# Attention and a mixture of experts: routed experts on gathered rows, expert work between attention slots

## The chip, the core and the metric

The kernel runs on one core of one Trainium2 chip. The metric is the device time of one execution in microseconds (us). Engines: PE multiplies matrices, DVE, ACT and POOL work element by element, SP issues DMAs.

## What is computed

The input is 4 batches of 1024 tokens, 256 wide (4096 tokens). Attention has 16 heads of 16; a query sees every key up to 64 places after itself. Each token then goes through a router that chooses 4 of 16 experts, and 2 shared experts.

```
x = layernorm(x + attention(x))              # 16 heads, key <= query + 64
scores = sigmoid(x @ router.T); sc = scores + bias
# 2 of 4 groups by the sum of their two best sc, then the 4 best experts in them
tw = scores[chosen] / sum * 2.5
routed = sum over chosen e of tw_e * (silu(x @ G_e.T) * (x @ U_e.T)) @ D_e.T   # 256 -> 128 -> 256
shared = (silu(x @ SG.T) * (x @ SU.T)) @ SD.T                                  # 256 -> 256 -> 256
out = layernorm(x + routed + shared)
```

## The kernel before

Matrix products at full precision are made of three products of 16-bit floats (high by high, high by low, low by high), with weights scaled by 64. Each engine has its own instruction list, and the lists meet at semaphores.

**Projection** (`project`, L631): eight chunks of 512 tokens. PE makes q, k and v (L647, L651); q and k are written to DRAM in two halves (L324) and read back in stacked form for each group of four heads (`stack`, L326 to L336). v stays in SBUF.

**Attention**: 16 groups (4 batches, 4 head groups), each of 13 slots (`SLOTS`, L34: a query half of 512 and a key tile of 128). In a slot PE makes the transposed scores of four heads (L587), ACT their exponential (L863), POOL cuts the masked corner (L509), and PE multiplies by v one slot later, four heads at once, in 32-bit floats (`weighted`, L604). Between them PE makes the untransposed scores of the next group (L572, L575), of which DVE takes row maxima (L984). The maxima are transposed (L616) and put into the q stack by a DMA, so that the exponential needs no bias. Scores have three PSUM banks, transposed scores three, P times V one, and transposes one (L252). The first part of `body` on every engine writes this order out by hand; `share` (L61) deals the score units to the slots. The weights of one expert are loaded and split in each group (L340, L853, L1010).

**Expert stage**: eight chunks of 512 tokens after all attention. All 18 experts are computed for all tokens: `up` (L750) makes gate and up in 12 matmuls of 512 columns each, ACT the silu (L940), DVE multiplies by the token's weight for that expert, which is 0 where it isn't chosen and comes broadcast from DRAM (L1185, L417), and by up (L1192); ACT and DVE split the result (L947, L1199); `down` (L764) adds 12 matmuls of 256 columns into two banks. The steps of the next chunk (`STEPS`, L283) stand between the experts: output projection (L680, L688), first norm, transposes (L696), logits (L704), routing (`route`, L1090, a chain of 30 small DVE operations, each waiting for the one before), and the transpose of the weights (L712). After the last expert come the residual (L1207) and the second norm. Loops over chunks and groups are hardware loops (`rounds`, L80).

## Time and profile before

| | |
|---|---|
| median of 3 runs | 1291.25 us (1289.18 to 1295.77) |
| profiled execution, span | 1287.9 us (3.35 below the median; its own device time is not listed) |
| instructions | 28066 |
| DMA | 76.78 MB, mean 60 GB/s |

The span runs from the first to the last instruction. Busy times of PE are not work at its peak, since matmuls are pipelined and their ends are modelled; spacing from start to start says more. The clock of PE is given as a share of 2.4 GHz.

### The profile page before, as it was taken

The page shows a single profiled execution, that of the slowest core. Times are in us where ns is not written, and L with a number is a line of the kernel's source. Part 1 is how long each engine was busy: PE and PEld are TensorE (multiplying, and loading weights), DVE is VectorE, ACT ScalarE, POOL GpSimd, SP SyncE. Part 2 cuts the span into 40 slices and gives each one's busy share as a digit, 9 for nine tenths or more (in the row PEclk, how much of TensorE's full clock was granted, in tenths as well). Part 3 has the DMA queues.
Part 4 walks back from the last instruction along what each step waited for, and adds up shares of the span by engine and source line. Part 5 has one row for each costly group of instructions (what it writes and reads, how often), then busy time and mean ns, then how long its engine had stood idle before and what let it go on. Part 6 is the DMA issues. An engine that isn't in the chain of part 4 may idle for free.

```text
span 1287.9 us, 28066 instructions
## 1 busy us (share of the span) xinstructions
PE 1214.8 (94%) x8448; PEld 644.6 (50%) x8448; DVE 947.5 (74%) x1975; ACT 625.9 (49%) x1366; POOL 238.9 (19%) x432
## 2 busy tenths in 40 slices
PE   7877999999999999999799999898998989989997
PEld 4543444444444444443356666565665656556564
DVE  7587888888888888887657776676776767757754
ACT  4415777777777777777633332323222232222332
POOL 8831222222222222222401010010200102000000
PEclk9998999999999999999999999898999999999999
DMA  5631111111111111110131232121312212122220
GB/s 166 187 116 53 38 39 39 37 37 37 37 37 37 37 34 32 34 36 14 46 84 61 48 99 59 61 71 43 90 49 63 77 51 90 50 47 77 59 82 33
DMA packets 62443, 76.78 MB, mean 60 GB/s; under 512 B 8992, under 2 KB 37408, under 8 KB 62368
## 3 DMA queue, kind: packets, MB, share of 16 engines
q1 hardware_dynamic: 60736, 72.80, 19.2%
q10 hardware_dynamic: 1632, 3.15, 0.8%
q8 instruction: 27, 0.44, 0.2%
q14 instruction: 48, 0.39, 0.1%
HBM read 62.94 MB, written 12.85 MB: 59 GB/s over the span
## 4 chain that ended last, share of the span: by engine, by line
PE 64%; DVE 13%; issue 9%; ACT 7%; SPq 2%; POOL 2%; DMA 2%; DVEq 0%; ACTq 0%; POOLq 0%
PE bank L759 16%; PE bank L604 11%; PE bank L572 9%; PE bank L587 9%; PE bank L772 9%; DVE hf L1192 3%; DVE sg L1185 3%; ACT hh L947 3%; ACT a_PT L863 3%; PE bank L647 2%; PE bank L575 2%; PE bank L688 1%; PE bank L628 1%; PE bank L651 1%; SPq L324 1%
## 5 line engine op out<-in xcount | busy, mean ns | idle before, releaser
L984 DVE TENSOR_REDUCE a_mx<-bank 128x1 f32<-128x512 f32 (+3 forms) x720 | 401.2, 618 | 73.7 <-PE bank L575 44.6
L863 ACT ACTIVATE a_PT<-bank 128x512 f32<-128x512 f32 (+4 forms) x832 | 357.0, 505 | 138.1 <-PE bank L587 137.5
L587 PE MATMUL bank<-a_QS,a_KS 113*128 113x512 f16 (+4 forms) x832 | 269.6, 331 | 11.4 <-ACT a_PT L863 6.1
L572 PE MATMUL bank<-a_KS,a_QS 112*128 112x512 f16 (+4 forms) x832 | 258.6, 332 | 15.5 <-DVE a_mx L984 8.3
L947 ACT CAST hh<-hf 128x512 f16<-128x512 f32 x144 | 89.0, 618 | 332.5 <-DVE hf L1192 332.5
L509 POOL TENSOR_SCALAR_AFFINE_SELECT a_PT<-a_PT 128x256 f32<-128x256 f32 (+1 forms) x288 | 109.6, 381 | 419.0 <-ACT a_PT L863 418.7
L604 PE MATMUL bank<-a_PT,a_VG 128*17 128x512 f32 (+4 forms) x1664 | 179.7, 504 | 6.4 <-POOL a_PT L509 6.4
L772 PE MATMUL bank<-dh,hh 128*128 128x256 f16 x576 | 159.0, 276 | 16.9 <-DVE z L1207 16.9
L1199 DVE TENSOR_TENSOR hl<-hf,hh 128x512 f16<-128x512 f32 x144 | 99.8, 693 | 99.4 <-ACT hh L947 99.4
L772 PE MATMUL bank<-dh,hl 128*128 128x256 f16 x576 | 159.1, 276 | 0.0
L772 PE MATMUL bank<-dl,hh 128*128 128x256 f16 x576 | 159.1, 276 | 0.0
L572 PEld LDWEIGHTS bank<-a_KS,a_QS 112*128 112x128 f16 x832 | 79.4, 98 | 114.6 <-DVE a_mx L984 84.2
L587 PEld LDWEIGHTS bank<-a_QS,a_KS 113*128 113x128 f16 x832 | 80.0, 98 | 109.4 <-ACT a_PT L863 54.8
L1192 DVE SCALAR_TENSOR_TENSOR hf<-bank,sg 128x512 f32<-128x512 f32 x144 | 99.5, 691 | 42.9 <-issue 28.5
L940 ACT ACTIVATE sg<-bank 128x512 f32<-128x512 f32 x144 | 85.6, 594 | 89.9 <-PE bank L759 89.9
L1185 DVE TENSOR_TENSOR sg<-sg,cb 128x512 f32<-128x512 f32 x128 | 91.0, 711 | 36.7 <-ACT sg L940 31.2
L575 PE MATMUL bank<-a_tri,a_idb 128*128 128x128 f16 (+1 forms) x576 | 111.3, 212 | 0.0
L523 POOL TENSOR_SCALAR ve<-mv 128x4 f32<-128x4 f32 x16 | 6.4, 402 | 545.2 <-DVE mv L1052 545.2
L759 PE MATMUL bank<-x1h,gh 128*128 (+1 forms) x288 | 87.3, 385 | 0.7 <-ACT cT L904 0.7
L759 PE MATMUL bank<-x1h,uh 128*128 (+1 forms) x288 | 86.0, 380 | 1.6 <-DVE hf L1192 1.6
L759 PE MATMUL bank<-x1l,gh 128*128 (+1 forms) x288 | 86.8, 384 | 0.0
L759 PE MATMUL bank<-x1h,gl 128*128 (+1 forms) x288 | 86.2, 381 | 0.0
(134 smaller groups left out, 1438.2 us busy)
## 6 DMA issues: line engine op xcount, KB each, us to landing
cb<-c_dram SPq DMA_DIRECT2D x128, 256.0 KB, 3.3
q_dram<-p_qk SPq DMA_DIRECT2D x32, 128.0 KB, 2.1
k_dram<-p_qk SPq DMA_DIRECT2D x32, 128.0 KB, 2.1
a_QS<-q_dram SPq DMA_DIRECT2D x64, 64.0 KB
a_KS<-k_dram SPq DMA_DIRECT2D x64, 64.0 KB
xb<-x SPq DMA_DIRECT2D x8, 512.0 KB, 3.6
out<-oo SPq DMA_DIRECT2D x8, 512.0 KB, 4.2
p_xf<-xT ACTq DMA_DIRECT2D x6, 512.0 KB, 4.2
```

The lines of the kernel that those rows point to most:

```text
L509: pool.affine_select(out=a, in_=a, compare_op=ALU.is_ge, fill=0.0, base=q0 - (kt * P - WIN), pattern=[[0, 2], [1, w]], channel_multiplier= ...
L572: mm = pe.matmul(bank[:, at:at + hi - lo], QS[p][0:MR, t // NT, h, t % NT * P:t % NT * P + P], KS[p][0:MR, piece, h % 2, 0:hi - lo], start ...
L575: mm = pe.matmul(bank[:, at + m0 - lo:at + hi - lo], idb[:], tri[:, m0 - P * t - WIN:m1 - P * t - WIN], start=False, stop=True)
L587: pe.matmul(stbank[u % 3][:, 0:(qc + 1) * CH - q0], KS[p][0:MR + 1, kt // NT, h % 2, kt % NT * P:kt % NT * P + P], QS[p][0:MR + 1, qc, h, ...
L604: mm = pe.matmul(otbank[32 * h:32 * h + HD + 1, q0 - qc * CH:CH], VG[p][:, kt, h:VW:HG], PT[(p + i) % 2][:, h, 0:(qc + 1) * CH - q0], star ...
L759: mm = pe.matmul(bank[:], ww[:, k, n, :], xx[:, k, bass.ds(t * CH, CH)], start=(i == 0), stop=(i == 5))
L772: mm = pe.matmul(y, a[n % NHB][:, j * P:j * P + P], w[:, n, :], start=(n == 0 and i == 0 and j % 2 == 0), stop=(n == NX - 1 and i == 2), s ...
L863: act.activation(PT[(p + i) % 2][:, h, 0:w], stbank[u % 3][:, 0:w], ACT.Exp)\
L947: act.copy(hh[n % NHB][:], hf[n % 2][:]).then_inc(f["hi_done"], 1)
L984: dve.tensor_reduce(mx[:, piece, t // NT, heads[0]:heads[0] + n, t % NT], sbank[u % 3][:, 0:n * w].rearrange("p (h k) -> p h k", h=n), AX. ...
L1185: dve.tensor_tensor(sg[n % 2][:], sg[n % 2][:], cb[e % NCB][:], op=ALU.mult)\
L1192: dve.scalar_tensor_tensor(hf[n % 2][:], ubank[n % 2][:], 1.0 / WSC, sg[n % 2][:], op0=ALU.mult, op1=ALU.mult).then_inc(f["h_done"], 1)
```

## The change

Only the order of the work and the routed experts change; projection and attention compute what they did, with v written to DRAM after the projection and read back per group.

**Order.** All hardware loops are unrolled. A function `plan` gives each engine a table of jobs by half slot (26 per attention group, 416 for all attention, 602 in all). PE takes at most one job in a half slot; the other engines may have several. A job is issued in the middle and at the end of each attention slot (`fill`). Batch b's side work begins at half slot 104 x (b + 1), when its attention is done; what is beyond 416 follows after attention. By the plan, preparation of batches 0 to 3 (output projection, norm, transposes, logits, routing, positions) stands at half slots 106 to 142, 210 to 246, 314 to 350 and 418 to 453; scatters at 143 to 163, 247 to 267, 351 to 371, 454 to 474; the 24 routed pairs at 170 to 269, 293 to 392, 421 to 486, 506 to 560; the 8 shared items at 125 to 146, 271 to 290, 396 to 414, 488 to 504; gathers at 282 to 302, 404 to 424, 498 to 518, 572 to 592. Pairs are three half slots apart within attention (more where PE's are taken) and two after it.

**Routed experts.** For each batch, `route` ends with the rank of each expert; PE counts positions by 44 matmuls with triangular and full matrices of ones; DVE (`place`, a chain of 18 operations) gives every token four row numbers, in expert order, each expert's rows padded to a multiple of 128: 48 units of 128 rows, whatever the routing. 32 indirect DMAs on POOL's queue write token rows (512 16-bit values, high and low part) to those rows in DRAM. Units are worked off in pairs: a transposing DMA loads 256 rows (256 KB, three buffers), PE reads the units' expert numbers into registers (8 at a time) and makes gate and up in 24 matmuls of 128 columns, weights addressed by register; ACT takes tanh, DVE makes the gated product in two operations, ACT and POOL split it, PE makes the output in 6 matmuls of 256 columns, ACT copies it out and SP stores it to DRAM (256 KB). 32 indirect DMAs on POOL's queue gather the four rows of each token, DVE adds them with their weights (32 dependent operations), and the second norm follows. Shared experts work on 256 tokens at a time with static weights.

**Memory.** The banks for scores and transposed scores become one ring of five taken in PE's order (0 to 4); P times V keeps bank 6, and banks 5 and 7 serve everything else; after attention a ring of seven serves all. Weights are loaded and split in the first six groups, three per group, by one operation each instead of three. `normal` scales four tiles in one operation instead of four.

The core of the diff:

```diff
+UNITS_B = TOPK * S // P + NE
+NPR = UNITS_B // 2
+NPS = NSH * NT
+NPB = NPR + NPS
...
+for b in range(B):
+    h0 = span * (b + 1)
+    for half in range(NH2):
+        c = b * NH2 + half
+        e = h0 + (2 if half == 0 else 7)
+        sp[e - 1].append(("load_res", c))
+        pool[e + 4].append(("add_bo", c))
+        o = e - 1
+        for k in range(KD):
+            o = put(("ont", c, k), o + 1)
+            act[o + 1].append(("oh", c, k))
+            dve[o + 2].append(("ol", c, k))
+        y = o + 2
+        for j in range(2):
+            y = put(("yo", c, j), y + 1)
+            dve[y + 1].append(("z", c, j))
+            dve[y + 2].append(("stats", c, j))
+        dve[y + 3].append(("aggr", c))
+        pool[y + 4].append(("rstd", c))
+        dve[y + 6].append(("norm", c))
+        act[y + 7].append(("row_hi", c))
+        pool[y + 8].append(("row_lo", c))
...
+q = -1
+for b in range(B):
+    for n in range(NPB):
+        shared = n < NPS
+        if shared:
+            h = ready[b * NH2 + n // NPS * NH2 + n // (NPS // 2)] if n else ready[b * NH2]
+            h = max(h, q + 2)
+        else:
+            h = max(routed[b] + 6, q + (3 if q < 2 * ATT else 2))
+        q = put(("gu", b, n), h)
+        act[q + 1].append(("tanh", b, n))
+        dve[q + 2].append(("gate", b, n))
+        act[q + 3].append(("hh", b, n))
+        pool[q + 4].append(("hl", b, n))
+        if not shared:
+            sp[q - 5].append(("load_rows", b, n))
+            y = put(("y", b, n), q + 6)
+            act[y + 1].append(("y_out", b, n))
+            sp[y + 3].append(("store_y", b, n))
+        elif n % NSH:
+            y = put(("ysh", b, n), q + 6)
+            dve[y + 1].append(("add_shared", b, n))
+    at = y + 6
+    for t in range(BT):
+        for k in range(TOPK):
+            pool[at + (t * TOPK + k) * 2 // 3].append(("gather", b, t, k))
+        w = at + (t * TOPK + TOPK) * 2 // 3 + 3
+        dve[w].append(("combine", b, t))
+        dve[w + 1].append(("stats2", b, t))
+        if t % NT == NT - 1:
+            c = b * NH2 + t // NT
+            dve[w + 2].append(("aggr2", c))
+            pool[w + 3].append(("rstd2", c))
+            dve[w + 4].append(("norm2", c))
+            sp[w + 5].append(("store", c))
...
+def take(ring, *job):
+    at = RINGS[ring][turn[ring] % len(RINGS[ring])]
+    turn[ring] += 1
+    if at in holder:
+        on.wait_ge(*emptied(holder[at]))
+    holder[at], bank_of[job] = job, at
+    return banks[at]
...
+        i = routed_nth(b, n)
+        u = 2 * (n - NPS)
+        if u % REGS == 0:
+            load_experts(b, u)
+        on.wait_ge(xt_loaded[i % 3], i // 3 * 16 + 16)
+        on.wait_ge(s["w_lo"], NX)
+        cols = [(experts[b, u + v], v * P, P,
+                 [(xt[i % 3][:, k, v * P:v * P + P], xt[i % 3][:, KD + k, v * P:v * P + P])
+                  for k in range(KD)]) for v in range(2)]
+    ps = take(ring, "gu", b, n)
+    for e, at, v, tall in cols:
+        for up in range(2):
+            i = 0
+            for lo, part in ((0, 0), (0, 1), (1, 0)):
+                for k in range(KD):
+                    mm = pe.matmul(ps[:, up * 2 * P + at:up * 2 * P + at + v],
+                                   weights(e, (2 * up + lo) * D + k * P, P), tall[k][part],
+                                   start=(i == 0), stop=(i == 5))
+                    i += 1
+    mm.then_inc(f["gu_ready"], 1)
+elif what == "y":
+    b, n = a
+    q, u = nth(b, n), 2 * (n - NPS)
+    on.wait_ge(f["hl_done"], q + 1)
+    ps = take(ring, "y", b, n)
+    for v in range(2):
+        e = experts[b, u + v]
+        for i, (o, at) in enumerate(((hh, 4 * D), (hh, 5 * D), (hl, 4 * D))):
+            mm = pe.matmul(ps[:, v * D:v * D + D], o[q % 4][:, v * P:v * P + P], weights(e, at, D),
+                           start=(i == 0), stop=(i == 2))
+    mm.then_inc(f["y_ready"], 1)
...
+sp.dma_start_transpose(xt[i % 3][:], rows[b % 2][at:at + 2 * P, :])\
+  .then_inc(xt_loaded[i % 3], 16)
...
+pool.indirect_dma_start(rows[b % 2], bass.IndirectOffsetOnAxis(ap=slot[b % 2][:, t, k:k + 1],
+                        axis=0), XR[:, t, :], None).then_inc(f["scattered"], 16)
...
+elif what == "gather":
+    b, t, k = a
+    i = b * BT + t
+    for n in range(3):
+        on.wait_ge(y_stored[n], (b + 1) * NPR // 3 * 16)
+    on.wait_ge(f["comb_done"], i - 1)
+    pool.indirect_dma_start(yg[i % 2][:, k, :], None, outs[b % 2], bass.IndirectOffsetOnAxis(
+        ap=slot[b % 2][:, t, k:k + 1], axis=0)).then_inc(gathered[i % 2], 16)
...
+elif what == "gate":
+    q = nth(*a)
+    ps = bank("gu", *a)
+    on.wait_ge(f["tanh_done"], q + 1)
+    dve.scalar_tensor_tensor(ga[q % 2][:], tq[q % 2][:], 1.0, ps[:, 0:2 * P], op0=ALU.add,
+                             op1=ALU.mult).then_inc(f["ga_done"], 1)
+    on.wait_ge(f["ga_done"], q + 1)
+    on.wait_ge(f["hl_done"], q - 1)
+    dve.scalar_tensor_tensor(hf[q % 2][:], ps[:, 2 * P:4 * P], 0.5 / WSC / WSC, ga[q % 2][:],
+                             op0=ALU.mult, op1=ALU.mult).then_inc(f["h_done"], 1)
...
+    ins = dve.scalar_tensor_tensor(zz, yg[i % 2][:, k, :], wk[b % 2][:, t, k:k + 1], zz,
+                                   op0=ALU.mult, op1=ALU.add)
+    ins.then_inc(f["comb_step"], 1)
+    on.wait_ge(f["comb_step"], i * TOPK + k + 1)
+dve.sem_inc(f["comb_done"], 1)
...
+for G in range(NR):
+    def some_scores(units):
...
+    for i in range(NSL):
+        rest, h2 = share(i), 2 * (G * NSL + i)
+        for h in range(HG):
+            scoresT(G, i, h)
+            some_scores(rest[h:h + 1] if h < HG - 1 else ())
+            if h == 1:
+                fill(h2)
+        if i:
+            weighted(G, i - 1)
+        some_scores(rest[HG - 1:])
+        if i == NSL - 1:
+            weighted(G, i)
+        fill(h2 + 1)
+for h in range(2 * ATT, END):
+    fill(h)
```

## Rows read from the trace of the kernel before

**Rows 1.** The page's busy line: busy us, share of the span, instructions per engine.

```profile
PE 1214.8 (94%) x8448; PEld 644.6 (50%) x8448; DVE 947.5 (74%) x1975; ACT 625.9 (49%) x1366; POOL 238.9 (19%) x432
```

**Rows 2.** Windows by stage: us; busy us (instructions) PE, PEld, DVE, ACT, POOL; clock, DMA, GB/s.

```profile
160.44:193.70 33.26, 32.80 (x257) 13.85 (x255) 27.64 (x60) 24.38 (x59) 7.25 (x19) 1.00 0.13 37
644.80:1287.90 643.10, 613.38 (x3936) 378.66 (x3936) 437.33 (x894) 198.63 (x360) 50.00 (x62) 0.98 0.23 65
```

**Rows 3.** Chain of waits in the expert stage: start us, us, what, how many.

```profile
656.63 1.31 PE bank L772 x12
657.94 0.87 PE bank L680 x8
658.82 2.59 PE bank L759 x12
...
662.72 2.62 PE bank L688 x24
...
685.71 0.59 PE bank L704 x24
```

**Rows 4.** PE in order of time, in the second attention group: start us, us, what.

```profile
195.21 0.22 PE L575 MATMUL bank<-a_tri,a_idb 128*128 128x128 f16 x1
195.27 0.38 PE L587 MATMUL bank<-a_QS,a_KS 113*128 113x512 f16 x1
195.58 1.07 PE L604 MATMUL bank<-a_PT,a_VG 128*17 128x512 f32 x8
196.58 0.31 PE L572 MATMUL bank<-a_KS,a_QS 112*128 112x320 f16 x1
```

**Rows 5.** DVE by line and form, 150 to 600 us: busy us, mean ns; idle before.

```profile
L984 DVE TENSOR_REDUCE a_mx<-bank 128x1 f32<-128x512 f32 x328 | 208.8, 683 | 38.7 <-PE bank L572 26.3 <-PE bank L575 12.4
```

**Rows 6.** Waits between 160 and 600 us: us in total, times, longest.

```profile
PEld bank L572 <- DVE a_mx L984: 64.8, 106, 0.8
```

**Rows 7.** SP's queue in order of time; the page's DMA issues (KB each, us to landing).

```profile
60.44 1.21 SPq L324 DMA_DIRECT2D k_dram<-p_qk  x2
68.50 0.75 SPq L334 DMA_DIRECT2D a_QS<-q_dram  x1
...
cb<-c_dram SPq DMA_DIRECT2D x128, 256.0 KB, 3.3
q_dram<-p_qk SPq DMA_DIRECT2D x32, 128.0 KB, 2.1
```

**Rows 8.** DVE in order of time: routing of chunk 0, and four statistics.

```profile
632.82 0.20 DVE L1105 TENSOR_SCALAR th<-th 128x64 f32<-128x64 f32 x1 [2.10 <-ACT th L899]
...
643.39 0.44 DVE L1141 SCALAR_TENSOR_TENSOR vm<-rank,th 128x64 f32<-128x64 f32 x1
...
828.00 1.40 DVE L1048 BATCH_NORM_STATS2 st<-z 128x6 f32<-128x256 f32 x4
```

**Rows 9.** DVE by line and form, 740 to 1200 us: 512 and 256 elements.

```profile
L1069 DVE SCALAR_TENSOR_TENSOR z<-bank,xb 128x512 f32<-128x512 f32 x12 | 7.7, 686 | 5.9 <-PE bank L688 5.9
...
L1207 DVE SCALAR_TENSOR_TENSOR z<-bank,o_all 128x256 f32<-128x256 f32 x20 | 7.1, 417 | 0.0
```

**Rows 10.** POOL by line and form: 150 to 600, 636 to 646, 740 to 1200 us.

```profile
L509 POOL TENSOR_SCALAR_AFFINE_SELECT a_PT<-a_PT 128x256 f32<-128x256 f32 x159 | 64.8, 408 | 110.9 <-ACT a_PT L863 110.9
...
L509 POOL TENSOR_SCALAR_AFFINE_SELECT a_PT<-a_PT 128x256 f32<-128x256 f32 x6 | 4.8, 830 | 2.2 <-ACT a_PT L863 2.2
...
L517 POOL TENSOR_TENSOR xb<-xb,bo 128x256 f32<-128x256 f32 x20 | 16.1, 835 | 0.0
```

**Rows 11.** Chain of waits during the projection: start us, us, what.

```profile
44.97 5.31 issue
...
103.55 4.30 DMA a_KS<-k_dram
```

**Rows 12.** Register operations on PE's queue at the logits: duration ns min/median/max.

```profile
L704 PEldq FUSED_REGOPS  x13: 46/46/51, 760.0 to 843.7; - x13
```

1583 lines of the change are left out of this document (850 added, 733 removed).

## Prediction

> **What bounds the kernel now.** I read the page's busy line first: PE 1214.8 of 1287.9 us, DVE 947.5 [rows 1]. Then the windows by stage. One attention group takes 33.3 us (16 of them, 108 to 642 us), with PE busy 32.8, DVE 27.6, ACT 24.4, POOL 7.3; the expert stage takes 643.1 us with PE busy 613.4 and DVE 437.3 [rows 2]. In the chain of waits of the expert stage PE hardly stops: an expert on 512 tokens costs 2.59 us up and 1.31 us down [rows 3], so 144 of them are 562 us, and the steps of the next chunk make up the rest. In attention PE streams too: a slot's P times V takes 1.00 us, and 128 columns cost 0.06 us from start to start [rows 4]; the score maxima on DVE are 683 ns for 512 columns [rows 5], and PE's weight loads wait 64.8 us of 440 for them [rows 6]. So PE leads in both stages, and in attention DVE is close behind (83%). That decides what follows: PE work is removed, but a large part of what stays is put where PE is already full and DVE nearly so.
>
> **The change, priced part by part.**
>
> *Expert arithmetic.* Routed experts shrink from 128 passes over 512 tokens to 96 pairs of 128-row units (24 per batch; 32 full units of work and 16 for the padding). A pair is 24 matmuls of 128 columns and 6 of 256. From 0.06 us and 1.31/12 = 0.109 us [rows 3, 4] that is 24 x 0.056 + 6 x 0.109 = 2.0 us. The 8 expert numbers that PE reads from memory once in four pairs are on no row. Below stands 0 (all hidden), above eight landings one after the other of 2.1 us, 17 us; a small read kept in the engine's own queue is nearest to an issue on SP, 0.75 us [rows 7], so I take 0.8 us, 0.2 per pair: 2.2 us a pair. That makes 96 x 2.2 = 211 us in place of 128 x 3.90 = 499. Shared experts stay 16 x 3.90 = 62 us, 15.6 per batch. The preparation of 1024 tokens is 2 x (0.87 + 2.62 + 0.87 + 0.59) = 9.9 us of PE [rows 3] (transposes, projection, transposes, logits), 11 with the 44 tiny matmuls for the positions.
>
> The Trainium skill ("TensorE: Matmul & The Clock Gate", Back-to-back issue gap) gives about 81 ns for a 128-column matmul in a stream with weight loads, where its isolated gap is 56. The trace speaks against it here: 24 pairs of weight load and 16-column matmul take 0.59 us [rows 3], so a weight load bounds nothing above 25 ns. By the page a pair would cost 0.6 us more, and the sum some 30 us more.
>
> *DVE per batch.* Preparation: Ol, z and x1l are 12 operations of 0.69 us [rows 9]; statistics and norm are 16 of 256 elements at 0.35 us from start to start [rows 8] and 8 small ones, 6.6 us. Two routings keep the chain up to the rank reduction, which ended 10.5 us after the start of the first of now 30 operations (632.82 to 643.39 [rows 8], 25 operations), and one more: 21.5 us. The 18 chained placing operations on up to 768 elements, by 1.05 ns an element and 0.15 us each (417 ns at 256, 686 at 512 [rows 9]), are 8.8 us. Together 45 us. A gate is two operations of 0.4 us: 24 pairs 19 us, 8 shared 6.4, with 2.8 for adding. Combining is 32 dependent operations at 0.44 us, 14 us, and the second norm 6.6. In all some 94 us per batch.
>
> *POOL and the indirect DMAs.* Per batch 32 operations hl of 0.83 us [rows 10] and 32 scatters and 32 gathers of 128 rows each. No row shows an indirect DMA. Bounds: SP spends 0.60 to 0.75 us to issue a direct one; from issue to landing 128 KB take 2.1 us [rows 7]. I take 1.0 us of POOL's queue for each, nearer to the issue, since the engine need not wait for the landing, but above it, since each row's address is worked out on POOL. Range 0.6 to 2.1.
>
> *Transposing loads* (96 of 256 KB) and the stores of y run in SP's queue beside the arithmetic; three buffers ahead. Bounds 0 and the 3.3 us of a 256 KB landing [rows 7], hidden by three buffers as long as each takes less than 3 x 2.2 us. I charge nothing; if the cover is gone, a rival below.
>
> *Start.* Without the loops the pause of 5.31 us in the projection's chain goes [rows 11]. The end of the start is bound by SP's queue and the a_KS landing at 103.55 + 4.30 [rows 11]. Ten weight loads move off that queue, one v store per chunk and one v load are added. I take 97 us in place of 108: the pause and 8 issues of 0.7 us go; bounds 92 and 110.
>
> *Attention with filling.* Engines work in order and PE runs at most five banks ahead, so stretches limited by different engines do not average: I take the largest per stretch. One half slot is 33.3/26 = 1.28 us, of which PE needs 97%, DVE 83%, POOL 0.28 us. By half slots of the plan:
> By half slots of the plan (a stretch of n bare ones is n x 1.28 us, times the engine's share; batch b's side work begins at 104 x (b + 1)):
> - 0 to 104, nothing of weight beside the groups: 133 us.
> - 104 to 143, preparation of batch 0 and 6 shared gates, DVE leads: 41 + 45 + 5 = 91.
> - 143 to 170, scatters: POOL 32 + 6 of masks in 20 half slots, then 7 bare ones, 9: 47.
> - 170 to 210, 11 pairs, PE leads: 50 + 24 = 74.
> - 210 to 247, preparation of batch 1 beside 5 to 7 pairs, DVE leads: 39 + 45 + 6 = 90.
> - 247 to 282, scatters, masks and 5 hl on POOL 42, then 15 half slots with shared experts, 27: 69.
> - 282 to 306, gathers of batch 0: POOL 32 + 6 + 6 for hl, then 5: 49.
> - 306 to 350, preparation of batch 2 and pairs, DVE leads: 47 + 45 + 7 = 99.
> - 350 to 371, scatters, POOL 43. 371 to 396, 7 pairs, PE 46. 396 to 416, shared experts, PE 39.
>
> The sum is 780 us in place of 534.
> The two rings of three banks become one of five: from nothing to 0.1 us in each of 208 slots (the wait for maxima, 64.8 us in 172 slots [rows 6], is 0.38 us per slot now); I take 8 us.
>
> *Tail after attention*, in the same way. All 24 pairs of batch 2 and all of batch 3 are still to do. Preparation of batch 3 with 8 pairs and the rest of batch 1's combining: DVE 45 + 13 + 6, 66 us with gaps. 32 scatters with 10 hl: 40. Six pairs and first shared: 17. Gathers of batch 2 with 10 hl: 40. 17 pairs: 37. Last y landing 4, 32 gathers 32, last combine, norm and store 12: 48. Sum 248 us.
>
> **The sum**: 97 + (780 + 8) + 248 = 1133 us of span. It is made against the profiled span of 1287.9; the median of the runs, 1291.25, lies 3.35 above it, which I add: 1136.
>
> **Rivals.**
> *A. The stretches average out.* PE and DVE queues absorb each other's bursts. Then attention is bound by the sum of DVE, 16 x 27.6 + about 250 = 692 us, with 4% of coupling 720, and POOL's tail overlaps a little more (230): 97 + 720 + 230 + 3 = 1050. For it speaks that the engines' queues already mix two streams at 98% of PE [rows 2]; against it the wait of 0.38 us per slot for maxima at DVE's present load [rows 6].
> *B. PE's pair costs more*, since each weight address comes from a register, and a pair has 28 of them. A register operation in PE's queue takes 46 ns [rows 12]: 1.3 us on top of 2.2. Of 96 pairs some 45 lie where PE leads: 60 us more, 1196. For it: 28 operations beside 60 dispatches in 2.0 us. Against it: logits with such addresses run at 25 ns a matmul [rows 3].
> *C. POOL becomes the bound* (the other side). An indirect DMA keeps POOL for c us; masks stand behind scatters in its queue, PE's P times V waits for the masks, and in the tail three rounds of 32 stand alone. 4.4 rounds in attention and 3 in the tail make 237 x (c - 1) us. It is slower than before from c = 1.65, and 1397 at c = 2.1. For it: masks of 256 elements took 830 ns instead of 408 while DVE did the routing [rows 10], and now eight routings and 128 combines stand near POOL's work. Against it: SP issues in 0.75.
> The Trainium skill ("SBUF — State Buffer", SBUF: two separate sides, and the section after it) says that GpSimd can't write its DMA descriptors while VectorE holds the port pair that both use, and has such a DMA go from some 0.62 to 3.1 us. By that figure for all of them the time would be some 1630 us, an estimate from that page. The slowed masks are of the same kind, at twice the time and not five times.
> *D. The transposing loads are slow.* Above 6.6 us each three buffers no longer hide them; at 8 us, 48 pairs in the tail at 8/3 or, if they don't overlap each other, at 8 us cost 48 x 5.8 = 278 us more: 1414. Slower than before from 5.3 us if they go one by one.
>
> **Chances.** Forecast 0.42, A 0.20, B 0.20, C 0.12 (0.08 of it beyond c = 1.65), D 0.06. A change within 0.5% (6.5 us, about what the three runs' spread of 6.6 us can tell) is left 0.03, the part of C around its point. Slower: 0.08 + 0.06 = 0.14. Faster: the rest, 0.83. Range: A with POOL's c a little under 1.0 reaches 1030 (24 us for 0.1); above it takes B with c at 1.3, 1196 + 71 = 1267, so 1270. That leaves some 0.03 below and 0.15 above.
>
> **What will show it.** The last P times V at about 885 us (97 + 788); indirect DMAs on POOL at 1.0 us from start to start; routed matmuls of 128 columns at 56 ns; group periods that alternate between 33 us at first, and 50 to 65 us where a batch is prepared; DVE above 90% in those, PE above 90% in the routed ones; PE sparse, and its clock at the lower level (1.2 GHz), while POOL scatters and gathers after attention. I am wrong if the period does not grow where batches are prepared (A), if PE's pairs stand over 3 us in a stretch without waits (B), if PE waits for masks or hl behind DMAs (C), or if pairs wait for xt (D).

## The result, and the profile after

The changed kernel takes 1379.27 us (median of 4 runs, 1376.3 to 1383.12) where the kernel before takes 1292.88 in the same job: 1.0678 times as long, interval 1.0648 to 1.0708. It is slower by 6.8%; forecast were 1136 us, range 1030 to 1270. The profiled execution has a span of 1374.6 us against 1287.9. The page's busy line, to be read beside [rows 1]:

```profile
PE 1034.1 (75%) x8592; PEld 603.9 (44%) x8592; DVE 867.9 (63%) x1832; ACT 595.9 (43%) x1361; POOL 582.5 (42%) x807
```

PE is busy for 181 us less. But its share of the span fell from 94% to 75%, and no other engine is full. So the gain went into waits. Where, the windows by stage say (columns as in [rows 2]): a group of attention without side work; half slots 104 to 143, 210 to 247 and 306 to 350 of the plan, in which a batch is prepared and routed; and all that is left behind attention:

```profile
188.70:226.50 37.80, 34.26 (x259) 13.98 (x262) 29.00 (x56) 26.07 (x60) 7.48 (x19) 1.00 0.73 240
263.90:374.70 110.80, 83.22 (x655) 45.29 (x658) 88.67 (x199) 48.21 (x111) 36.14 (x49) 0.85 0.18 50
521.30:634.20 112.90, 84.01 (x727) 49.19 (x727) 81.85 (x188) 46.10 (x108) 35.22 (x49) 0.85 0.28 57
795.90:920.70 124.80, 94.67 (x845) 55.55 (x844) 93.72 (x212) 55.87 (x132) 40.35 (x63) 0.88 0.33 69
1051.00:1374.60 323.60, 183.18 (x1792) 150.21 (x1792) 159.23 (x380) 75.19 (x174) 168.62 (x195) 0.75 0.55 132
```

In the three preparations PE is busy 74 to 76% and DVE 72 to 80%, at a granted clock of 0.85 to 0.88, where a bare group has 1.00. In the first of the three both are busy at once for only 62.6 of 110.8 us, PE alone for 20.6, DVE alone for 26.0, neither for 1.5; in the others both are busy for 55.6 of 112.9 and 66.2 of 124.8. So neither engine leads; they take turns. The waits of the first preparation between the two (us in total, times, longest) are in the main these:

```profile
DVE a_mx L1095 <- PE bank L461: 12.3, 9, 3.6
DVE a_mx L1095 <- PE bank L458: 6.3, 4, 2.8
PE bank L656 <- DVE e_hf L1327: 6.0, 2, 4.8
PE bank L631 <- DVE e_hf L1327: 4.8, 2, 2.7
PE bank L580 <- DVE e_hf L1327: 3.7, 1, 3.7
```

DVE's waits for PE's scores make 18.6 us, PE's for DVE all of its 27.6 us of idle time; e_hf is the gated product of an expert pair, x1l the low half of the normed tokens.

The plan's stretches against the forecast (from the first P times V of a slot to that of another, read in order of time), with two runs from further down. The one without routing also leaves out the indirect DMAs and the reading of expert numbers; of the last version the slowest of four executions was profiled (1273.38 us, the median is 1265.84). By the mark used here the start of the kernel before takes 110.6 us, where the forecast counts 108.

```
us                 forecast  changed  no routing  last version
start                    97    115.6       115.3         115.9
half slots 0-104        133    148.3       147.5         148.4
104-143                  91    110.8        81.1         100.5
143-170                  47     60.6        45.6          46.1
170-210                  74     86.0        76.6          75.7
210-247                  90    112.9        79.2         100.2
247-306                 118    161.7       148.3         137.5
306-350                  99    124.8        93.8         133.6
350-416                 128    130.2       114.4         116.1
rings                     8        -           -             -
behind attention        248    323.6       208.8         297.5
span                   1133   1374.6      1110.6        1271.6
```

How PE and DVE take turns is seen on PE in order of time, at the start of a preparation (in brackets idle time before it, and what ended it):

```profile
305.03 0.96 PE L487 MATMUL bank<-a_PT,a_VG 128*17 128x448 f32 x8
309.68 1.11 PE L580 MATMUL bank<-a_ident,e_R 128*128 128x128 f32 x4 [3.69 <-DVE e_hf L1327]
...
311.33 0.63 PE L458 MATMUL bank<-a_KS,a_QS 112*128 112x512 f16 x1
314.68 0.61 PE L631 MATMUL bank<-e_x1h,a_W 128*128 128x256 f16 x2 [2.71 <-DVE e_x1l L1313]
```

and on DVE in the same microseconds:

```profile
304.36 0.26 DVE L1163 TENSOR_SCALAR e_th<-e_th 128x64 f32<-128x64 f32 x1
...
309.20 0.42 DVE L1327 SCALAR_TENSOR_TENSOR e_hf<-bank,e_ga 128x256 f32<-128x256 f32 x1
311.42 0.69 DVE L1095 TENSOR_REDUCE a_mx<-bank 128x1 f32<-128x512 f32 x1 [1.79 <-PE bank L458]
...
313.93 0.69 DVE L1313 TENSOR_TENSOR e_x1l<-bank,e_x1h 128x512 f16<-128x512 f32 x1
```

The transposes of L580 need one of the two banks that all side work shares, and that bank is free only when DVE has made e_hf from it (L1327). That stands behind 13 routing operations, which began at 304.36, and two maxima. PE is idle for 3.69 us; when it goes on, DVE in turn waits 1.79 us for the scores that PE could not make meanwhile. The next pause has the same shape, with x1l (L1313).

A pair of routed units, in the tail:

```profile
1265.80 1.64 PE L631 MATMUL bank<-e_xt,a_W 128*128 128x128 f16 x23
...
1268.12 2.17 PE L631 MATMUL bank<-e_xt,a_W 128*128 128x128 f16 x24
...
1270.86 0.27 PE L644 MATMUL bank<-a_W,e_hl 128*128 x1
1274.30 0.93 PE L631 MATMUL bank<-e_xt,a_W 128*128 128x128 f16 x8 [3.17 <-issue]
```

One pair takes 2.85 us (from 1268.12 on, the last of its 30 matmuls 0.11 us behind 1270.86), and every four pairs PE stands 3.2 us for "issue", so that a pair costs 3.6. What its queue does in that time is no matmul; by line:

```profile
L535 PEldq FUSED_REGOPS  x192: 146/146/165, 425.6 to 1302.7; - x192
L535 PEldq SEQ_ASSERT  x192: 18/18/24, 425.8 to 1302.9; - x192
L535 PEldq TENSOR_LOAD <-e_expert x24: 587/592/1120, 424.8 to 1299.9; - x24
```

This is the reading of eight expert numbers, each compared with its bound. The same operation as in [rows 12] now stands before two in three of the weight loads of the gate and up matmuls (2304 in all), 46 ns each:

```profile
L631 PEldq FUSED_REGOPS  x1536: 46/46/51, 428.0 to 1313.5; - x192
```

POOL's indirect DMAs (duration min/median/max in ns):

```profile
L916 POOL DMA_INDIRECT rows<-e_XR,e_slot x128: 956/961/1866, 359.0 to 1176.8; - x128
...
L931 POOL DMA_INDIRECT a_pool<-outs,e_slot x128: 940/947/1232, 709.3 to 1361.8; - x128
```

With 31.6 us of issue in 124 places before L916, one comes every 1.25 us. What stood behind them in POOL's queue shows in the waits (us in total, times, longest; a_PT L883 is the masking of the corner, e_hl the low half of the gated product):

```profile
PEld bank L487 <- POOL a_PT L883: 35.3, 29, 5.1
PE bank L644 <- POOL e_hl L923: 28.7, 19, 7.8
...
PE bank L656 <- POOL e_hl L923: 18.7, 5, 4.7
```

At the start the pause of [rows 11] is gone, but in its place the chain of waits runs through the round trip of V by DRAM, and a_KS lands 5 us later than before:

```profile
32.63 5.02 DMA v_dram<-p_vs
...
100.72 3.24 DMA v_dram<-p_vs
108.10 4.74 DMA a_KS<-k_dram
```

### The profile page after: what moved, and what is told of

It reads as the page before. It is cut to its first block, busy times and chain, and to the rows that moved or that the text cites. A ratio compares the mean times of both kernels' runs of the same rounds, so it can differ in the third digit from the quotient of the medians.

```text
span 1374.6 us, 25464 instructions
## 1 busy us (share of the span) xinstructions
PE 1034.1 (75%) x8592; PEld 603.9 (44%) x8592; DVE 867.9 (63%) x1832; ACT 595.9 (43%) x1361; POOL 582.5 (42%) x807
## 4 chain that ended last, share of the span: by engine, by line
PE 40%; DVE 20%; POOL 18%; issue 13%; DMA 3%; SPq 2%; ACT 2%; POOLq 0%; DVEq 0%
PE bank L631 10%; PE bank L487 8%; PE bank L471 7%; POOL a_pool L931 7%; DVE a_mx L1095 6%; PE bank L458 6%; POOL rows L916 6%; PE bank L644 4%; POOL e_hl L923 2%; POOL a_PT L883 2%; DVE e_R L1345 2%; ACT a_PT L992 1%; PE bank L461 1%; SPq L717 1%; PE bank L517 1%
## 5 line engine op out<-in xcount | busy, mean ns | idle before, releaser
L471 PE MATMUL bank<-a_QS,a_KS 113*128 113x512 f16 (+4 forms) x832 | 283.8, 349 | 25.4 <-DVE a_mx L1095 18.8
L883 POOL TENSOR_SCALAR_AFFINE_SELECT a_PT<-a_PT 128x256 f32<-128x256 f32 (+1 forms) x288 | 114.2, 402 | 396.1 <-ACT a_PT L992 395.5
L458 PE MATMUL bank<-a_KS,a_QS 112*128 112x512 f16 (+4 forms) x832 | 270.0, 346 | 12.5 <-DMA a_KS<-k_dram 6.1
L631 PE MATMUL bank<-e_xt,a_W 128*128 128x128 f16 x2304 | 198.0, 244 | 53.2 <-issue 36.3
L631 PEld LDWEIGHTS bank<-e_xt,a_W 128*128 x2304 | 171.8, 109 | 82.6 <-issue 65.0
L923 POOL TENSOR_TENSOR e_hl<-e_hf,e_hh 128x256 f16<-128x256 f32 x128 | 94.1, 736 | 198.6 <-ACT e_hh L1050 197.7
L916 POOL DMA_INDIRECT rows<-e_XR,e_slot x128 | 127.2, 994 | 57.7 <-issue 31.6
L931 POOL DMA_INDIRECT a_pool<-outs,e_slot x128 | 124.1, 970 | 60.5 <-issue 30.5
L471 PEld LDWEIGHTS bank<-a_QS,a_KS 113*128 113x128 f16 x832 | 84.0, 102 | 115.1 <-DVE a_mx L1095 52.9
L458 PEld LDWEIGHTS bank<-a_KS,a_QS 112*128 112x128 f16 x832 | 82.8, 102 | 106.2 <-ACT a_PT L992 64.8
L644 PE MATMUL bank<-a_W,e_hh 128*128 x384 | 80.3, 305 | 61.3 <-POOL e_hl L923 28.7
L1323 DVE SCALAR_TENSOR_TENSOR e_ga<-e_tq,bank 128x256 f32<-128x256 f32 x128 | 53.2, 416 | 104.5 <-ACT e_tq L1043 101.4
L1345 DVE SCALAR_TENSOR_TENSOR e_R<-a_pool,e_wk,e_R 128x256 f32<-128x256 f32 x128 | 69.0, 539 | 44.9 <-DMA a_pool<-outs,e_slot 41.4
L1056 ACT ACTIVATE e_ys<-bank 128x512 f32<-128x512 f32 x96 | 57.5, 599 | 40.4 <-PE bank L644 40.2
L461 PEld LDWEIGHTS bank<-a_tri,a_idb 128*128 128x128 f16 x576 | 57.6, 103 | 31.9 <-issue 9.6
```

Of the source, the lines that this page charges most:

```text
L458: mm = pe.matmul(ps[:, at:at + hi - lo], QS[p][0:MR, t // NT, h, t % NT * P:t % NT * P + P], KS[p][0:MR, piece, h % 2, 0:hi - lo], start=T ...
L461: mm = pe.matmul(ps[:, at + m0 - lo:at + hi - lo], idb[:], tri[:, m0 - P * t - WIN:m1 - P * t - WIN], start=False, stop=True)
L471: pe.matmul(ps[:, 0:(qc + 1) * CH - q0], KS[p][0:MR + 1, kt // NT, h % 2, kt % NT * P:kt % NT * P + P], QS[p][0:MR + 1, qc, h, q0 - qc * C ...
L631: mm = pe.matmul(ps[:, up * 2 * P + at:up * 2 * P + at + v], weights(e, (2 * up + lo) * D + k * P, P), tall[k][part], start=(i == 0), stop ...
L644: mm = pe.matmul(ps[:, v * D:v * D + D], o[q % 4][:, v * P:v * P + P], weights(e, at, D), start=(i == 0), stop=(i == 2))
L883: pool.affine_select(out=a, in_=a, compare_op=ALU.is_ge, fill=0.0, base=q0 - (kt * P - WIN), pattern=[[0, 2], [1, w]], channel_multiplier= ...
```

## The experiments

The trace left three theories. S: PE's side jobs wait for DVE work that stands behind routing in DVE's queue, with two banks for all of them. W: routing is vector work that is paid for in full, however it is placed. C (P in the two runs on the pace of the DMAs; in another expectation P stands for PE as the bound): POOL's indirect DMAs set the pace of what stands behind them. Each kernel was timed in three rounds beside the kernel before (medians of that one: 1289.3 to 1291.5 us). Ratios are to the kernel before, so that the runs of different jobs can be compared; the changed kernel is at 1.0678.

### What each part costs

**Expert numbers.** In `load_experts`:

```diff
-    _, regs = nc.values_load_multi_w_load_instructions(expert[b % 2][0:1, n:n + REGS], ...)
-    for i, e in enumerate(regs):
-        experts[b, n + i] = e
+    for i in range(REGS):
+        experts[b, n + i] = (n + i) % NE
```

> The expert numbers are fixed at build time (unit n uses expert n mod 16), so the load of the numbers into PE's registers, its bounds checks and the address arithmetic per weight load are left out. Theory PE (rival B: the dear routed pair is what the forecast missed): in the changed kernel a pair takes 2.0 us up and 0.8 us down with register addresses, where 1.34 and 0.65 were forecast, and each group of four pairs pays 3.4 us for the load; 96 x 0.9 + 24 x 3.4 = 165 us less PE work, of which at least half is on the path: 1300 us or less. Theory order (the five engines hold each other up in a fixed order, and PE's own work is seldom what ends last): under 50 us, 1330 us or more.

1340.4 us, ratio 1.0369 (1.033 to 1.0407): 39 us, as theory order had it, not PE. A pair takes 2.01 us in its trace (1257.23 to 1259.24 below), as the forecast's 2.0 had it:

```profile
1257.23 1.51 PE L629 MATMUL bank<-e_xt,a_W 128*128 128x128 f16 x24 [0.45 <-DMA e_xt<-rows]
...
1259.24 1.50 PE L629 MATMUL bank<-e_xt,a_W 128*128 128x128 f16 x24
```

So addresses from registers cost 0.85 us a pair and the reading of numbers another 0.8, of which the forecast had 0.2.

**Indirect DMAs.** Scatters and gathers replaced by the bare signal:

```diff
-    pool.indirect_dma_start(rows[b % 2], ..., XR[:, t, :], None).then_inc(f["scattered"], 16)
+    pool.sem_inc(f["scattered"], 16)
-    pool.indirect_dma_start(yg[i % 2][:, k, :], None, outs[b % 2], ...).then_inc(gathered[i % 2], 16)
+    pool.sem_inc(gathered[i % 2], 16)
```

> Scatters and gathers are left out (POOL only counts the semaphores up), so experts work on the zeros in the row buffer and the sum takes what lies in the buffer. Theory POOL (rival C: scatters and gathers at 1.27 us from start to start, 0.98 busy and 0.27 issue, hold the masks and the hl operations up): 7.4 rounds of 32 x 1.27 = 300 us of POOL, of which each round hides at most what the others need, some 22 us: 1379 - 7.4 x 20 = about 1230 us. Theory PE: POOL only fills time that PE's dear pairs need anyway, 1340 us or more.

1294.69 us, 1.0019 (0.9998 to 1.004): 85 us, of them 60 in the tail (323.6 to 263.7). That lies between the two theories. PE's wait for masks falls from 35.3 to 18.7 us and that for e_hl from 28.7 to 6.8.

**Transposing loads.** `dma_start_transpose` became a plain `dma_start` of the same bytes (what the pairs then multiply is not transposed).

> The transposing loads become plain loads of the same 256 KB (the transposition of the gathered rows is left out). Theory D (slow transposing loads): PE waits for them in the tail, 48 pairs by several us: 1280 us or less. All others: within 15 us of the changed kernel, 1365 to 1385 us; SP's issue falls from 1.3 to 0.7 us, which is off the path.

1397.71 us, 1.0819 (1.079 to 1.0848): nothing to gain there. It came out 18 us slower, which neither side expected.

**All of these and routing.** Fixed numbers, no indirect DMAs, and routing and placing left out but for one copy and two fills:

```diff
-    (26 operations per chunk in route, 18 per batch in place)
+    dve.memset(M[:, j0:j0 + NT, :], 0.0).then_inc(f["rank_done"], 1)
+    dve.memset(wk[b % 2][:], 0.0).then_inc(f["wk_done"], 1)
```

> Leaves out the routing and the placing on the vector engine (two small fills and one copy stand for them), all 256 indirect DMAs, and the loading of expert numbers, which are fixed when the kernel is built; every matmul, load, gate and combination is still done. With the second and first experiment (1294.69 and 1340.4 us) it says how much of the change is paid for choosing and moving tokens and how much for the pairs themselves. If what each leaves out adds up, no indirect DMAs (-84) and fixed numbers (-39) give 1256; theory W (routing fills the vector engine in the half slots 104 to 143, 210 to 247 and 306 to 350, 349 us against 147 before): another 60 to 100 us off, 1160 to 1200. Theory M (the pairs' own matmuls, gates and transposing loads fill these half slots): within 20 us of 1256.

> Leaves out the 256 indirect DMAs and fixes the expert numbers when the kernel is built; routing and placing are still computed. It stands between the run without the indirect DMAs (1294.69 us) and the one that also leaves routing out (1108.86). If the prices add up (39 us for the numbers), 1256 us, and routing and placing then cost 147 us, more than the 119 us of vector work that they are. If TensorE bounds what is left once POOL is relieved, the numbers cost more than 39 here: 1210 to 1240.

Without routing 1108.86 us, 0.8585 (0.8562 to 0.8608), below all that was expected. With routing, but with fixed numbers and no indirect DMAs, 1219.97, 0.9449 (0.9417 to 0.948). The prices don't add up: fixed numbers give 39 us alone and 75 beside relieved POOL. And routing costs 111 us (1219.97 - 1108.86) where its own DVE time is 858.4 - 748.7 = 110 us. The preparation 104 to 143, first with routing, then without:

```profile
264.40:376.80 112.40, 83.35 (x651) 44.88 (x650) 88.46 (x198) 48.03 (x110) 30.55 (x44) 0.85 0.16 43
```

```profile
262.80:343.90 81.10, 72.04 (x651) 40.90 (x650) 60.82 (x131) 47.25 (x110) 26.66 (x44) 0.98 0.21 59
```

DVE has 27.6 us more to do, the stretch takes 31.3 longer, and PE's same 651 instructions are busy for 83.4 in place of 72.0 us: the granted clock went from 0.98 to 0.85 as PE came to stand idle. None of the routing is hidden, though DVE is at 79%. Together with it, though, its chain of dependent steps was left out, on which scatters and pairs wait; the pair of runs doesn't tell the two apart.

### In what way routing costs

**Banks.** Two rings for the scores, `"scores": [0, 1, 2], "scoresT": [3, 4]`; then six banks for the first four groups and one for the rest of their work:

```diff
-RINGS = {"scores": [0, 1, 2, 3, 4],
+RINGS = {"scores": [0, 1, 2, 3, 4], "early": [0, 1, 2], "earlyT": [3, 4, 5], "one": [7],
```

> Same computation; scores get a ring of banks 0 to 2 of their own and transposed scores banks 3 and 4, in place of one ring of five in PE's order. Theory ring: in the first groups, which have no side work, the period grew from 33.3 to 37 us because transposed scores now wait for maxima on DVE and scores for exponentials; with rings of their own it falls to 34 us or less there, and the time by 16 x 3 = 50 us, to 1330. Rival (the DMA traffic and the weight splits of the first groups did it): period stays at 36 us or more, time within 10 us of 1379.

> Same computation. In the first four attention groups, where no routed work runs, the scores get six banks in two rings of three, as the kernel before has them, and everything else one bank; from the fifth group on it is the changed kernel. Theory B (the lost bank and the shared ring cost the 37.4 us per group against 33.3): the first four groups fall from 148.3 to 134 to 138 us, the run to about 1366. Theory D (it is the three weight splits of a group and the 48 fills of 256 KB, which both kernels do not have alike): the first four groups stay at 145 to 150, the run within 5 us of 1379.

1404.78 us, 1.0871 (1.0843 to 1.0899), and 1419.42, 1.0988 (1.0965 to 1.1012). With six banks the first three groups take 35.8, 34.5 and 36.7 us in place of 36.8, 36.3 and 37.8, but the fourth, before the switch to the other rings, 47.1. Less than half of what a bare group lost (33.3 to 37) is the bank; the rest was not isolated. That this run takes another 37 us behind half slot 247 I can't explain. With two rings the first group stays at 37.3 us, so theory ring failed; the time, 1404.78, is outside its rival's range too.

**Order in a half slot.** DVE issues all else ahead of `route` and `place`.

```diff
-for what, *a in DVE_AT.get(h, ()):
+for what, *a in sorted(DVE_AT.get(h, ()), key=lambda job: job[0] in ("route", "place")):
```

> Same computation; only the order inside a half slot changes: the vector engine issues its gate, transposing-split and combining work ahead of the routing and placing pieces that were planned for the same half slot. Theory S (TensorE's side jobs wait for vector work that stands behind a routing piece in the vector engine's queue, with only two banks for all side jobs, so that the two engines take turns): the half slots 104 to 143, 210 to 247 and 306 to 350, 349 us in the changed kernel, lose 20 to 50 us and the run comes out at 1330 to 1360 us against 1379. Theory W (the vector engine is simply full there, and the order is of no matter): within 5 us of 1379. Theory C (POOL's indirect DMAs set the pace of the half slots behind): within 10 us of 1379, or slower, since routing ends later.

1393.3 us, 1.0811 (1.0764 to 1.0858). The first two preparations gained 5 us each, the third 2, where theory S had 20 to 50 together, and more was lost behind them. In the first, PE's waits for e_hf fell from 14.5 to 7.7 us, but those of its attention matmuls (L458, L471) for the maxima rose from 2.5 to 13.6: the order moves the wait from one job to another.

**Finer pieces.** Ten pieces for a chunk's routing, nine for a batch's placing:

```diff
-            for n in range(5):
-                dve[g + 2 + n].append(("route", c, n))
+            at = max(g + 2, last + 1)
+            for n, m in enumerate([4, 3, 6, 3, 4, 1, 1, 1, 1, 2] if b < B - 1 else [7, 6, 7, 2, 4]):
+                last = at + n
+                dve[last].append(("route", c, m))
```

> Same computation. For the first three batches the routing of a chunk (26 vector instructions) is handed out in ten pieces over ten half slots instead of five over five, with the long comparisons alone, and the placing (18 instructions) in nine instead of four; the second chunk's routing starts after the first's, and scatters and routed pairs begin about 13 half slots later. Theory S2 (a routing piece of 2 to 3 us stops the maxima for longer than the five scores banks last, so that TensorE stands still; pieces of at most 1.4 us would pass): most of the price of routing in attention comes back, 1290 to 1340 us. Theory W (the vector work is paid for in full however it is cut, because the stretches have TensorE and vector work one behind the other): within 10 us of 1379.

1441.63 us, 1.1157 (1.1112 to 1.1202): the largest miss. Half slots 104 to 170 take 167.6 us where they took 171.4: what the preparation gained stood 13 half slots later, beside the scatters. 247 to 282 went from 80.9 to 112.3 and the tail from 323.6 to 363.7. Cutting routing up didn't hide it here, though the edit also put scatters and pairs 13 half slots later, and the two effects were not run apart.

**Numbers without comparisons**, alone and on the finer pieces: `skip_runtime_bounds_check_because=...` in the load.

> Same computation; the 24 loads of eight expert numbers each no longer compare every number with its bound on TensorE's sequencer (0.28 us a number by the trace, 2.2 us a load, 53 us over the run), the load itself (1.04 us) and the addresses from registers stay. Theory P (TensorE bounds the tail and much of the attention behind half slot 104): 1335 to 1360 us, of it 10 to 18 us in the tail. Theory C (POOL and the vector engine set the pace of attention): the tail alone gains, 1360 to 1370. Fixed numbers gave 1340.4, which is the floor of this one.

> Same computation; the finer pieces of the run before and the expert numbers loaded without their comparisons together. If the vector engine's pieces were what hid the comparisons' price in the run that left them out (1386.6 us), this one is 15 to 40 us faster than the finer pieces alone; if the comparisons cost nothing on the path, within 8 us of it.

1386.59 us, 1.074 (1.0721 to 1.0759), and 1410.02, 1.0924 (1.0883 to 1.0966): 7 us slower the one time, outside both theories, and 32 us faster than the finer pieces the other. In the first, pairs at the end of the tail follow each other every 3.0 us, and the longest wait for issue is 1.2 us in place of 3.2, yet the tail stays at 323.1: in it the gate and up matmuls waited for issue 28 times (19.3 us) in place of 11 (23.1 us), and PE's output matmuls another 13 times (11.8 us).

**Less DVE work.** The eight largest values of 16 by one instruction per 128 tokens, in place of the comparison of all pairs:

```diff
-link(dve.tensor_tensor(gt[:], one, two, op=ALU.is_gt))
-link(dve.tensor_tensor(eq[:], one, two, op=ALU.is_equal))
+for j in range(NT):
+    link(dve.max(top[:, j0 + j, :], vm[:, j, :]))
...
-link(dve.tensor_reduce(rc, gt[:], AX.X, ALU.add))
-link(dve.tensor_scalar(M[:, j0:j0 + NT, :], rc, float(TOPK), None, op0=ALU.is_lt))
+link(dve.tensor_tensor(is_k[:, j0:j0 + NT], vm ..., top[:, j0:j0 + NT, 0:TOPK] ..., op=ALU.is_equal))
+link(dve.tensor_tensor(M[:, j0:j0 + NT, :], vm[:], top[:, j0:j0 + NT, TOPK - 1:TOPK] ..., op=ALU.is_ge))
```

> Same result by a shorter way: the four best experts of a token come from the vector engine's instruction for the eight largest values (one on 16 values for every 128 tokens) and two comparisons with them, in place of two comparisons of all pairs, a product, a sum and a reduction over 1024 elements each, and of the comparison of ranks in the placing. By the rows of the changed kernel this takes 46 us of vector work away (10.5, 11.4, 5.4, 5.9, 9.8 and 3.2) and adds 5 to 8. Theory W (routing costs its vector time one for one, since PE and vector work follow each other in the preparation stretches): 40 us less, 1335 to 1350. Theory L (it costs by its chain of waits, the steps' number, which falls only from 44 to 43 per chunk and batch): within 12 us of 1379.

1368.55 us, 1.0592 (1.0556 to 1.0628): 11 us, in the range of theory L (the chain's length) and not of W. DVE's time fell by 40.8 us (867.9 to 827.1); a 16-element maximum costs next to nothing:

```profile
L1190 DVE MAX8 e_top<-e_vm 128x8 f32<-128x16 f32 x32 | 5.6, 176 | 0.9
```

The three preparations of attention gained 24.5 us together (110.8 to 101.7, 112.9 to 105.9, 124.8 to 116.4), but half slots 247 to 306 took 12 us more. That stretch was 161.7 us in the changed kernel, and 172 to 177 in six runs, none of which was meant to lengthen it (plain loads, two rings, gate first, six banks, no comparisons, this one). So one edit's gain stands against 10 us and more by which work falls into place elsewhere, and differences of this size between two kernels, though far outside the spread of their runs, can't be put down to the edit. In the preparations theory W holds nearly (three batches' share of the 40.8 us is 31, and 24.5 came back); over the whole run it failed.

### In what way the indirect DMAs cost, and a version that is faster

```diff
+ hi2, lo2: max and min of s4[..., 0:2] and s4[..., 2:4]; the two best = max(hi + hi, max(hi + lo))
-for what, *a in POOL_AT.get(h, ()):
+for what, *a in sorted(POOL_AT.get(h, ()), key=lambda job: job[0] in ("scatter", "gather")):
```

> The eight largest values as in the run before, the sum of a group's two best in six steps in place of eleven, the expert numbers loaded without their comparisons, and on POOL the low half of h ahead of a half slot's indirect DMAs. Theory W: another 8 us of vector work less, and with the vector engine relieved the comparisons' price shows (31 us in the pair of runs with finer pieces): 1295 to 1325 us. If the comparisons stay hidden as in the run with them alone: 1325 to 1340.

1329.37 us, 1.0278 (1.0233 to 1.0324), 39 us less than the run before. That is the range for comparisons that stay hidden, not that of theory W. The three edits added in it were not run one by one on this base.

Then the pace of the indirect DMAs, by the plan alone: one per half slot where the plan had three in two. The first of two runs does it for the last batch's scatters and the other batches' gathers; the second adds the scatters of the other batches. The gathers of the last batch keep their pace.

```diff
-pool[q + 5 + (t * TOPK + k) * 2 // 3].append(("scatter", b, t, k))
+pool[q + 5 + (t * TOPK + k) * 2 // (2 if b == B - 1 else 3)].append(("scatter", b, t, k))
-pool[at + (t * TOPK + k) * 2 // 3].append(("gather", b, t, k))
+pool[at + (t * TOPK + k) * 2 // (2 if b < B - 1 else 3)].append(("gather", b, t, k))
```

> As the run before, with the scatters of the last batch and the gathers of the first three at one per half slot in place of one and a half. Theory P (the indirect DMAs cost through POOL's pace: at one and a half per half slot POOL needs 1.9 us for them, and masks and the low half of h stand behind): 15 to 30 us less than the run before. Theory N (only their number counts): within 6 us of it.

> As the run before, and the first three batches' scatters at one per half slot too, which starts the routed pairs 11 half slots later. Theory P: the stretches 143 to 170, 247 to 282 and 350 to 371 lose 10 to 20 us together, but up to 15 us come back in the tail, where four more pairs of batch 2 then stand: between 15 us faster and 5 us slower than the run before. Theory N: 10 to 15 us slower, by the later pairs alone.

1300.38 us, 1.0073 (1.0043 to 1.0104): 29 us for the same 256 DMAs; 3 of them stand ahead of half slot 282, where the edit begins. PE's wait for e_hl falls from 25.0 to 17.5 us and for masks from 38.1 to 27.0. With the scatters paced as well 1304.56 us, 1.0108 (1.008 to 1.0136): attention ends 21 us earlier (988 us), and the tail takes 18 more (309.8). Both times lie in theory P's range (pace), and not in that of N (number alone).

The tail was then the largest stretch with idle engines. The third batch's pairs (batch 2, counted from 0) stood between the steps of the last batch's preparation, on which scatters, pairs and gathers wait in turn. They were moved behind it:

```diff
+            if not shared and b == B - 2 and h > 2 * ATT:
+                h = max(h, pos_at[B - 1] - 6)
             q = put(("gu", b, n), h)
```

> As the run with the paced tail (1300.38 us), and behind attention the third batch's routed pairs start six half slots before the last batch's positions are counted, in place of between its preparation's steps; its gathers go at two per three half slots. Theory K (the tail is a chain: preparation, scatters, pairs, gathers; the pairs between the preparation's steps lengthen its first link, 70 us, and fit beside the scatters anyway): the tail falls from 292 to 265 to 280 us, 1275 to 1290. Theory O (the tail is work, only its order changes): within 6 us of 1300, or slower, since TensorE idles more in the preparation.

> The same edit on the run with all indirect DMAs at one per half slot (1304.56 us, attention ended at 988 us, tail 310). Theory K: its tail was longer by 18 us since more of the second batch's gathers and the shared experts fell into the preparation; with the pairs out of the way it falls to 270 to 290: 1260 to 1283. Theory O: within 6 us of 1304.

On the first of the two bases 1283.11 us, 0.9942 (0.9922 to 0.9962); on the second 1265.84 us, 0.979 (0.9757 to 0.9823). **The last one is faster than the kernel before**, by 2.1% in the median, though the interval leaves open whether it is 2%, and faster than the change as it was made by 8.3% (0.979 / 1.0678 = 0.917).

Both times lie in theory K's ranges, but the traces don't show its mechanism:

```
us                                     first base  reordered  second base  reordered
last P times V of attention                1009.9      991.8        988.5      974.3
from there to the last batch's scatters      69.8       67.3         82.9       80.1
to its first pair                            76.7       84.1         82.4       81.3
to its last gate and up matmul               84.0       75.0         83.5       75.1
to the end                                   60.8       61.0         60.8       60.8
span                                       1301.2     1279.2       1298.1     1271.6
```

Attention ended 18 and 14 us earlier, although the edit changes no entry of the plan before half slot 416 on the first base and 431 on the second: with the same jobs in the same places attention took another time, and why is open. In the tails, 291.4 and 309.6 us before the edit, 287.4 and 297.3 after it, the preparation became only 2.5 to 3 us shorter, and theory K's tails (265 to 280 and 270 to 290) were not reached. The last batch's pairs gained 8 to 9 us; the third batch's gathers, which stand beside them, had also been given a slower pace, and that was not run alone. So of the 26.5 us between the two spans on the second base the edit doesn't explain 14, half of what puts the last version ahead of the kernel before. The last version's tail in four windows (preparation with the second batch's gathers; third batch's pairs beside the scatters; the last batch's; final gathers):

```profile
974.10:1036.00 61.90, 33.35 (x308) 27.65 (x308) 53.12 (x129) 10.79 (x24) 49.10 (x54) 0.72 0.38 91
1036.00:1130.00 94.00, 75.01 (x776) 59.59 (x777) 39.74 (x100) 33.78 (x80) 53.27 (x65) 0.91 0.75 178
1130.00:1210.00 80.00, 71.94 (x756) 56.47 (x754) 51.62 (x112) 30.94 (x74) 50.82 (x61) 0.96 0.98 210
1210.00:1271.60 61.60, 3.33 (x30) 2.14 (x28) 23.20 (x58) 2.37 (x5) 34.78 (x38) 0.56 0.33 102
```

and the changed kernel's, cut at the like points:

```profile
1051.00:1130.00 79.00, 46.53 (x462) 37.46 (x463) 65.69 (x160) 16.89 (x37) 37.05 (x44) 0.72 0.38 93
1130.00:1220.00 90.00, 63.16 (x602) 52.17 (x599) 28.38 (x64) 26.72 (x64) 57.59 (x66) 0.84 0.66 159
1220.00:1321.00 101.00, 73.48 (x732) 60.58 (x732) 42.82 (x102) 31.59 (x73) 40.39 (x52) 0.82 0.70 157
1321.00:1374.60 53.60, 0.00 (x0) 0.00 (x0) 22.34 (x56) 0.00 (x0) 33.59 (x36) 0.50 0.33 98
```

Against the changed kernel the preparation is 17 us shorter, with less routing, other pacing and the new order together, and in the pairs' two windows PE is busy 84% of 174 us where it was 72% of 191. The last 54 to 62 us, gathers with TensorE idle, are in both.

## Why the prediction was wrong

**The step that failed** is the one that let two engines' work overlap: "Engines work in order and PE runs at most five banks ahead, so stretches limited by different engines do not average: I take the largest per stretch." Taking the largest assumes that within a stretch the two engines overlap in full. The sums behind it were good: 41 + 45 + 5 = 91 us of DVE for 104 to 143 were 88.7, 90 for 210 to 247 were 81.9, 99 for 306 to 350 were 93.7. But with five banks for the scores, two for all side work and every queue in order, these stretches didn't take the larger of the two engines' times; they took 1.25, 1.38 and 1.33 times DVE's, 348.5 us where 280 were forecast: 69 us in these three alone. DVE, which was to be above 90% busy in them, was at 72 to 80%. The waits show the two engines standing still for each other in turn, and leaving routing out (110 us of DVE work and its chain) takes 111 us off the end. Which of the three conditions decides, the two banks for side work, the order of the queues or the length of the chain, stays open: changing the order or the pieces gave nothing in all, the run with 41 us less of DVE work and almost the same chain gave 11, and more banks for side work were not tried. Part of it is TensorE's clock, which the forecast had expected to fall only behind attention: with gaps in PE's work it was granted 0.85 in the preparations, and the same matmuls took 11 us more in one of them.

**The tail**, 248 forecast and 323.6 measured, was made of the same kind of maxima: 66 us for the preparation were 79 (1051 to 1130); scatters, six pairs and shared experts 57 were 90; gathers beside 17 pairs and the remaining pairs 77 were 101; the last gathers 48 were 54. Leaving the indirect DMAs out took 60 us off the tail, fixed expert numbers some 22. That the pairs between the preparation's steps lengthened it was an idea of mine that the reordered runs bear out by 2.5 to 3 us only.

**The pair**, 2.2 us, was 3.6 where nothing else bound it (2.85 and the pause). Rival B had 3.5 us, all of it for register operations; they cost 0.85, and the other 0.8 is the reading of the numbers, which the forecast had at 0.2. Leaving both out gave 39 us alone, 75 without the indirect DMAs, where B had 60. The argument against it, 25 ns a matmul with such addresses in the logits [rows 3], was misread: there are 13 register operations in all between 760 and 844 us [rows 12] for the 48 matmuls of two chunks, so each serves about four.

The Trainium skill's figure for a 128-column matmul behind a weight load ("TensorE: Matmul & The Clock Gate", Back-to-back issue gap), 81 ns, was set against the trace in the prediction. With fixed addresses 24 of them took 1.35 us (from 1257.23 to the next instruction at 1258.58), 56 ns each, so the trace stands. In the changed kernel the median of the pairs without a pause among their 24 is 1.99 us, 83 ns each, but there by the register operations.

**POOL**: 1.0 us per indirect DMA was 0.96 busy and 1.25 from start to start. Rival C's formula, 237 x (c - 1), gives 59 us at 1.25, and the point at which it decides, 1.65, was not reached. Leaving the DMAs out gives 85 us, but takes away what the forecast had charged for them too, so that it doesn't measure the 59; pacing them gave 29. Rival C acted as its text had it, through masks (and e_hl) that stood behind the DMAs, far below its break-even. Of the rule in the Trainium skill that GpSimd can't write DMA descriptors while VectorE holds the shared port pair ("SBUF — State Buffer", SBUF: two separate sides, and the section after it), with 0.62 to 3.1 us, the trace shows little: the median is 0.96, the longest 1.87.

**Rival D** fell (plain loads gained nothing), and so did **rival A**, of which this is the opposite: the stretches overlapped less than the sum of maxima assumes, not more. **The start** was forecast at 97 (bounds 92 to 110) and took 115.6: V's round trip took the place of the pause. **Groups without side work** were carried over at 33.3 us and took 37.1 (148.3 in place of 133). The merged rings were priced at 8 us, 0.5 a group, and cost some 1.3 each in the groups without side work (six banks gave back 3.9 us in three groups). The other 2.5 us a group may be the added weight splits and zero fills; that was not tried.

The three parts, 18.6 at the start, 147.4 in attention (935.4 against 788) and 75.6 behind it, make the 241.6 us between 1133 and 1374.6.

## What to carry to other kernels

When side work is put between the steps of a loop that keeps two engines at 80 to 97%, don't take the larger engine's time per stretch: with a few shared banks and queues in order it was 1.25 to 1.4 times that, and TensorE's clock fell as well. Leaving out 110 us of routing gave 111 back, but making it 41 us shorter gave only 11: shortening a part is not worth its busy time either. Look in the trace for pauses that alternate (PE behind DVE, then DVE behind PE). Slow instructions that nobody waits for (indirect DMAs here) belong on the plan at a pace that their queue can serve together with what others wait for. And where two engines wait for each other, compare stretches that the edit doesn't touch before believing a gain: here they moved by 10 to 18 us between kernels without an edit to them.

## What the runs showed of the hardware

- Granted clock and gaps: 0.98 and 0.85 for the same 651 TensorE instructions, with 9 and 29 us of idle time in the stretch.
- A weight load whose address comes from a register follows the one before after 107 ns in the median, 121 to 125 in most places of the pair at 1268.12, where a register operation stands between, 56 ns where not. A read of eight numbers into registers with comparisons keeps PE idle for 3.2 us at a time; without them the longest wait for issue is 1.2.
- An indirect DMA of 128 rows keeps POOL for 0.94 to 0.96 us, and the next starts 1.25 to 1.27 us after its start. The issue of a transposing load of 256 KB takes 1.3 us of SP's queue:

```profile
L787 SPq DMA_TRANSPOSE e_xt<-rows x96: 1227/1295/3167, 421.4 to 1305.9; - x96
```

- The instruction for the eight largest of 16 values takes 176 ns on 128 partitions.
